# Phase 2 on row tiles with rings of four; residual and biases written to banks; new orders on all engines

## The reference

```python
# block 1: attention by exponential features, 16 heads of 8
q, k, v = split_heads(x@Wq.T+bq), split_heads(x@Wk.T+bk), split_heads(x@Wv.T+bv)
f = lambda t: exp((t/sqrt(8))@R - 0.5*sum((t/sqrt(8))**2))
out = einsum(f(q), einsum(f(k), v), 1/(sum(f(q)) + 1e-8)) @ Wo.T + bo
# block 2: 16 slots ask x, one expert per slot, then x asks the slots
o = slot + mha(slot, x, x; d_*)                       # 16 heads, 256 keys
h = layernorm(o)*g + b                                # each slot its own g, b
o = o + (silu(h@W1+b1) * silu(h@Wg+bg)) @ W2 + b2     # each slot its own weights
out = mha(x, o, o; c_*)                               # 16 heads, 16 keys
```

## Time and profile before

| | us |
|---|---|
| median of 3 runs | 195.14 (194.88 to 195.6) |
| profiled execution | 194.75 |
| its span in the trace | 193.0 |
| TensorE busy | 179.7 (93%) |
| GpSimd busy | 146.3 (76%) |
| VectorE busy | 141.6 (73%) |
| ScalarE busy | 116.6 (60%) |

### The profile page before, as it was taken

The page is one execution under the profiler, slowest core; times in us unless marked ns, Lnnn a source line. Parts: engine busy times, 40 slices in busy tenths (PEclk is TensorE's granted clock), DMA queues, the critical chain, the costliest instruction groups (busy, mean ns, idle before and its releaser), DMA issues.

```text
span 193.0 us, 4707 instructions
## 1 busy us (share of the span) xinstructions
PE 179.7 (93%) x1439; PEld 136.6 (71%) x1439; DVE 141.6 (73%) x413; ACT 116.6 (60%) x296; POOL 146.3 (76%) x286
## 2 busy tenths in 40 slices
PE   0898789999999999999999999999999799999993
PEld 0445477777876687777788767523777699999993
DVE  2669968788877887869785743655448999999961
ACT  2235367796688857867966675446334465666561
POOL 4498969879699985999277693317947999999960
PEclk9999999999999999999999999999999999999999
DMA  4739957999990000000000000000000001111122
GB/s 108 240 102 366 360 147 257 349 362 327 372 298 13 0 3 2 3 0 3 0 3 0 2 5 0 3 0 0 3 0 0 3 27 54 58 58 54 38 75 82
DMA packets 19674, 18.24 MB, mean 95 GB/s; under 512 B 1289, under 2 KB 15458, under 8 KB 19650
## 3 DMA queue, kind: packets, MB, share of 16 engines
q1 hardware_dynamic: 18802, 17.35, 28.3%
q10 hardware_dynamic: 848, 0.59, 1.1%
HBM read 15.84 MB, written 2.10 MB: 93 GB/s over the span
## 4 chain that ended last, share of the span: by engine, by line
PE 80%; POOL 11%; DMA 3%; DVE 2%; issue 1%; ACTq 1%; ACT 1%; POOLq 0%; DVEq 0%
PE ps L1061 11%; PE ps L1133 7%; PE ps L1328 7%; PE ps L1300 7%; PE ps L1183 4%; PE ps L1171 4%; PE ps L1241 4%; PE ps L1114 4%; PE ps L1071 4%; PE ps L1318 4%; PE ps L1094 3%; PE ps L1309 3%; PE ps L1084 3%; DMA X<-in_L_attn_x_dram 3%; PE ps L1125 2%; PE ps L1104 2%
## 5 line engine op out<-in xcount | busy, mean ns | idle before, releaser
L1061 PE MATMUL ps<-Wproj,xnT 128*128 128x512 f32 x64 | 32.5, 633 | 0.9 <-ACT Wproj L515 0.5
L481 POOL TENSOR_TENSOR pr<-ft,rsm 128x256 f32<-128x256 f32 x32 | 19.3, 625 | 0.9 <-DVE rsm L970 0.9
L1061 PEld LDWEIGHTS ps<-Wproj,xnT 128*128 128x128 f32 x64 | 11.4, 198 | 9.9 <-issue 8.6
L1133 PE MATMUL ps<-XN2T,Ad 128*128 128x256 f32 x64 | 16.7, 384 | 0.1
L1328 PE MATMUL ps<-sq,prT 128*128 128x128 f32 x128 | 16.8, 275 | 0.0
L1300 PE MATMUL ps<-xnT,XN2T 128*128 128x256 f32 x64 | 16.5, 383 | 0.0
L429 POOL TENSOR_SCALAR xn<-X,nm,rs 128x127 f32<-128x127 f32 x32 | 14.7, 468 | 1.5
L1328 PEld LDWEIGHTS ps<-sq,prT 128*128 128x128 f32 x128 | 15.5, 192 | 0.0
L794 DVE TENSOR_REDUCE ss<-sq 128x64 f32<-128x512 f32 x16 | 10.9, 678 | 5.8 <-ACT sq L555 5.7
L654 ACT ACTIVATE ft<-ex 128x512 f32<-128x512 f32 x16 | 10.1, 630 | 8.3 <-POOL pr L481 7.1
L548 ACT ACTIVATE pr<-ps,nmax 128x256 f32<-128x256 f32 x32 | 14.9, 474 | 0.3 <-DVE nmax L833 0.2
(11 more groups left out here) (178 smaller groups left out, 508.6 us busy)
## 6 DMA issues: line engine op xcount, KB each, us to landing
W1s<-in_L_ffn_e_W_dram SPq DMA_DIRECT2D x4, 1024.0 KB, 8.0
Wgs<-in_L_ffn_e_Wg_dram SPq DMA_DIRECT2D x4, 1024.0 KB, 8.3
W2s<-in_L_ffn_e_W_dram SPq DMA_DIRECT2D x16, 256.0 KB, 8.3
out_dram<-V2s SPq DMA_DIRECT2D x16, 128.0 KB, 1.7
X<-in_L_attn_x_dram SPq DMA_DIRECT2D x3, 512.0 KB, 6.1
X<-in_L_attn_x_dram ACTq DMA_DIRECT2D x2, 128.0 KB, 2.6
X<-in_L_attn_x_dram ACTq DMA_DIRECT2D x1, 256.0 KB, 4.9
W<-in_L_ffn_e_b_dram SPq DMA_DIRECT2D x3, 32.0 KB, 1.8
```

The source lines that it names most:

```text
L481: last = pool.tensor_tensor(heads(at[:, k, j * HS:(j + 1) * HS], S), heads(ep[:, k, j * HS:(j + 1) * HS], S), over(rsm[:, k, j * H:(j + 1) ...
L1061: last = pe.matmul(banks(b)[:, j, :], xnT[:, k, j * P:(j + 1) * P], Wproj[:, :], start=True, stop=True)
L1133: last = pe.matmul(ps[:, 4, hf * NT:(hf + 1) * NT], Ad[:, hf * P:(hf + 1) * P], XN2T[:, b, :], start=True, stop=True)
```

## The change

- **Phase 2** no longer steps in lockstep: each engine has a written order of calls over blocks, and the buffers are rings of four (RING), laid into the experts' weights, which are no longer needed by then.
- The queries are projected for blocks 0 to 3 only. For the others the weights are folded: key_weights multiplies WqT by the packed keys of six blocks at a time, four row tiles of 32 partitions, each into a bank of its own, and the scores take XN2T as it is with the result KW.
- Values: value_weights does the same for four blocks at a time (VSET), 16 products of 32 partitions to 64 columns of the array each, in place of BDv @ W[CO] block by block. GpSimd packs keys and values (pack_keys, pack_values) instead of spreading them, and spreads keys only for blocks 1 to 3.
- The residual add of phase 2 is split: ScalarE copies the outputs (keep_outputs), GpSimd adds X (add_kept); only block 15 is still added by VectorE. VectorE also does half of the last scaling (scale_last).
- Keys: VectorE makes the first block straight from the bank (first_keys); ScalarE keeps the rest.
- slot + d_bo is written to banks 0 and 1 by VectorE from loaded copies; three of the eight hidden biases are copied to their banks by ScalarE (set_bias). The loads for that stand on SP behind the experts' weights.
- key_values makes only the four diagonal 32x32 tiles, and mask_kv spreads them.
- No negated means; 1e-8 is a ninth element of each head in ft, summed with the others.
- TensorE begins with products of the identity (warm). The orders of all engines in phase 1 are new.

The diff, cut to its core (the long lines of calls in full only for phase 2 and the start):

```diff
-QUERIES1 = 6
-QUERIES2 = 11
+QUERIES2 = 4
+KEY_SETS = ((QUERIES2, (QUERIES2 + NB) // 2), ((QUERIES2 + NB) // 2, NB))
+BANK_KW = (0, 1, 6, 7)
+RING = 4
+VSET = NB // 4
+BY_DVE = (15,)
...
-            rstd1(0); rstd1(1); apply1(1); rstd1(3); apply1(2); apply1(3); slot_rows(); other_masks(); add_bias(0)
-            add_bias(1); scale_features(0); add_bias(2); rstd1(5); scale_features(1); apply1(4); add_bias(3)
+            rstd1(0); rstd1(1); apply1(1); rstd1(3); apply1(2); apply1(3); scale_features(0); rstd1(5)
+            other_masks(); add_bias(0); add_bias(1); add_bias(2); apply1(4); scale_features(1); rstd2(0); apply2(0)
...
+            def in_tiles(to, what, mask, first, end):
+
+                return pool.tensor_tensor(to[:, first:end, :].rearrange("p b (h s) -> p b h s", s=S),
+                                          what[:, :, first:end].rearrange("p s b -> p b s").unsqueeze(2)
+                                          .broadcast_to([P, end - first, EG, S]),
+                                          mask[:, :].unsqueeze(1).unsqueeze(3).broadcast_to([P, end - first, EG, S]),
+                                          ALU.mult)
...
+            spread_keys(1); pack_keys(0); spread_keys(2); spread_keys(3); pack_keys(1); scale2(0); pack_values(0)
+            scale2(1); pack_values(1); pack_values(2); scale2(2); add_kept(0); add_kept(1); scale2(3); scale2(4)
...
-                sc.activation(ft[:, b % 2], ex[:, b % 2], ACT.Exp).then_inc(ft_ok, 1)
+                sc.activation(ft[:, b % 2, :, :, 0:DH], ex[:, b % 2].rearrange("p j (h d) -> p j h d", d=DH),
+                              ACT.Exp).then_inc(ft_ok, 1)
...
+            def set_bias(n):
+
+                i = 5 + n
+                sc.wait_ge(sg_ok, i - 4)
+                sc.activation(ps[:, BANK_UP[i], :], hbias[:, n, :], ACT.Copy).then_inc(bias_set, 1)
+
+            sc.wait_ge(h_in, 16 * 3 * EG)
+            tanh(0, 0); tanh(0, 1); tanh(1, 0); set_bias(0); tanh(1, 1); set_bias(1); tanh(2, 0); set_bias(2)
+            tanh(2, 1); act_columns(0); tanh(3, 0); act_columns(1); tanh(3, 1); act_columns(2); act_columns(3)
...
+            def slots_residual():
+
+                ve.wait_ge(slots_in, 16 * EG)
+                ve.wait_ge(ex_ok, NB)
+                for half in range(2):
+                    last = ve.tensor_tensor(ps[:, half, 0:2 * P].rearrange("p (g d) -> p g d", g=2),
+                                            slotr[:, 2 * half:2 * half + 2, :], under(d_bo_all[:, :], 2), ALU.add)
+                last.then_inc(slots_set, 1)
...
+            first_keys(); maxima2(0); shift2(0); maxima2(1); shift2(1); sums2(0); maxima2(2); norms2(0); shift2(2)
...
+            def warm(n):
+
+                pe.wait_ge(ident_ok, 1)
+                for _ in range(n):
+                    pe.matmul(ps[:, 2, 0:P], ident[:, :], ident[:, :], start=True, stop=True)
...
-                pe.matmul(ps[:, 6, NT:NT + P], WvP[:, :], gT[:, b % 2, :], start=True, stop=True).then_inc(kv_ok, 1)
+                for r in range(EG):
+                    last = pe.matmul(ps[r * Q:(r + 1) * Q, 6, NT:NT + Q], WvP[:, r * Q:(r + 1) * Q],
+                                     gT[:, b % 2, r * Q:(r + 1) * Q], start=True, stop=True)
+                last.then_inc(kv_ok, 1)
...
+            warm(5); turn_biases(); warm(1); turn_weights(); feature_weights(); warm(1); turn_xn(0)
+            turn_value_weights(); warm(1); project(0); turn_xn(1); project(1); key_sums(0); turn_xn(2)
...
+            def key_weights(c):
+
+                first, end = KEY_SETS[c]
+                pe.wait_ge(tile_k_ok, c + 1)
+                wait(pe, kw_ok, 2 * c)
+                for r in range(EG):
+                    tile = slice(r * Q, (r + 1) * Q)
+                    last = pe.matmul(ps[:, BANK_KW[r], 0:(end - first) * 64], WqT[tile, :],
+                                     tile_k[tile, first:end, :].rearrange("p b m -> p (b m)"), start=True, stop=True)
+                last.then_inc(kwp_ok, 1)
+
+            def value_weights(g):
+
+                pe.wait_ge(tile_v_ok, g + 1)
+                pe.wait_ge(kw_ok, 4)
+                wait(pe, vw_ok, g)
+                for i in range(VSET):
+                    for r in range(EG):
+                        tile = slice(r * Q, (r + 1) * Q)
+                        last = pe.matmul(ps[(r % 2) * 64:(r % 2) * 64 + 64, r // 2, i * P:(i + 1) * P],
+                                         tile_v[tile, g * VSET + i, :], W[tile, CO, :], start=True, stop=True)
+                last.then_inc(vwp_ok, 1)
...
+            scores2(0); scores2(1); key_weights(0); scores2(2); scores2(3); key_weights(1); scores2(4); turn_at(0)
+            value_weights(0); turn_at(1); scores2(5); outputs2(0); scores2(6); outputs2(1); turn_at(2)
+            value_weights(1); scores2(7); outputs2(2); turn_at(3); scores2(8); turn_at(4); outputs2(3); scores2(9)
```

More of the change, by code:

```diff
@@ L623, in _ @@
+            keep_slots(13); exp_scores(14); keep_xn2(15); keep_slot_values(14); keep_prT(14); keep_slots(14)
+            exp_scores(15); keep_slot_values(15); keep_prT(15); keep_slots(15); part2()
+            for b in range(QUERIES2):
                 keep_queries(b)
@@ L881, in _ @@
-            slot_outputs(2); maxima(15); slot_weights_of_sums(3); slot_heads(3); slot_outputs(3)
-            slot_weights_of_sums(4); slot_heads(4); slot_outputs(4)
+            stats1(0); moments1(0); center_weights(); set_biases(); spread_rotation(); stats1(1); apply_first()
+            center_values(); moments1(1); stats1(2); stats1(3); moments1(2); moments1(3); stats1(4); moments1(4)
+            norms_sq(0); exponents(0); stats1(5); moments1(5); sums(0); norms(0); norms_sq(1); exponents(1)
@@ L1220, in _ @@
                 last.then_inc(o_ok, 1)
-            for b in range(QUERIES1, QUERIES2):
+            for b in range(QUERIES2):
                 queries(b)
@@ L1238, in experts_in @@
                 pe.wait_ge(hT_ok, 1 + g // 2)
+                wait(pe, bias_set, 2 * g + u - 4)
                 w = (W1s, Wgs)[u]
@@ L1333, in _, with scores2 @@
-            for t in range(STEPS2):
-                step2(t)
-                if t == 3:
-                    for b in range(QUERIES2 + 3, NB):
-                        queries(b)
+            slot_keys_values(1)
+            def scores2(b):
+                if b == 0:
+                    pe.wait_ge(bdk0_ok, 1)
+                    pe.wait_ge(q2_ok, QUERIES2)
+                elif b < QUERIES2:
+                    pe.wait_ge(bdk_ok, b)
+                else:
+                    pe.wait_ge(kw_ok, 2 if b < KEY_SETS[0][1] else 4)
+                wait(pe, sx_ok, b - 1)
+                keys = BDk[:, b, :] if b < QUERIES2 else KW[:, :, b, :]
+                for j in range(2):
+                    last = pe.matmul(ps[:, 2 + b % 2, j * HS:(j + 1) * HS], XN2T[:, b, j * P:(j + 1) * P],
+                                     keys, start=True, stop=True)
+                last.then_inc(sp_ok, 1)
@@ new lines, in turn_at @@
+            def turn_at(b):
+                wait(pe, at_ok, b + 1)
+                if b == NB - 1:
+                    pe.wait_ge(at_last, 1)
+                wait(pe, atT_ok, b - 1)
+                for j in range(2):
+                    for hf in range(2):
+                        last = pe.transpose(ps[:, 4 + b % 2, hf * NT + j * P:hf * NT + (j + 1) * P],
+                                            at[:, b % RING, j * HS + hf * P:j * HS + (hf + 1) * P], ident[:, :])
+                last.then_inc(tt_ok, 1)
@@ new lines, in outputs2 @@
+            def outputs2(b):
+                wait(pe, atT_ok, b + 1)
+                pe.wait_ge(vw_ok, b // VSET + 1)
+                if b >= 2:
+                    on_dve = b - 2 in BY_DVE
+                    pe.wait_ge(ob_dve if on_dve else oc_ok, done(b - 2, on_dve))
+                for j in range(2):
+                    for hf in range(2):
+                        last = pe.matmul(ps[:, 6 + b % 2, j * P:(j + 1) * P], atT[:, b % RING, hf, j * P:(j + 1) * P],
+                                         VWs[:, hf, b, :], start=(hf == 0), stop=(hf == 1))
+                last.then_inc(op_ok, 1)
```

568 lines of the change are left out of this document (274 added, 294 removed).

## The result

The changed kernel takes **202.2 us** (median of 4 runs, 202.1 to 202.33); the kernel before, beside it, 195.06 (194.88 to 195.6). The ratio is 1.036, with an interval of 1.034 to 1.037: slower by 3.6%, where 186.5 was forecast. The profiled execution took 202.33, its span is 200.6.

What follows compares the result with a forecast made beforehand. TensorE was taken to bound phase 1 and lead phase 2, with VectorE and GpSimd close. 194.75 - 3.5 + 0.4 - 2.1 - 0.2 - 0.35 - 2.85 = 186.15, as a median 186.5 us; range 183 to 192.

Steps and rivals of the forecast that it cites:

- Startup: First 26 us: GpSimd and VectorE work removed, identity products added, exponents(2) moved ahead; 3.5 us gained, bounds 1 to 5.2.
- Rival B: Phase 2: row tiles gain nothing, six sets cost 20.5 us instead of 6.0; 201 us, slower; chance 0.06.
- 1 of clock: Start: earlier TensorE work puts part of the first project at the fast level; 1 us taken, of 0 to 1.8.
- 2.5 of idle: Start: exponents(2) ahead of center_slot_weights and residual(0) lets project(3) start sooner; 2.5 us of TensorE's idle time gained.
- Phase 1, steady, +0.4: 26 to 110 us, TensorE full: key-value column tiles cost 0.16 us more alone, 0.04 less beside slots; +0.4 in all.
- rival D: Phase 1: reading ft in runs of eight slows key_sums by up to 7 us; 193.5 us; chance 0.05.
- From the last slots to the experts, -2.1: Last slot_outputs to turn_xh(0): output product 1.55 us earlier and one query fewer, so turn_xh(0) starts 2.1 us earlier.
- The query, -0.6: Behind the output product: one query product fewer ahead of turn_xh(0), saving about 0.6 us.
- Experts and into phase 2, -0.55: turn_xh(0) to scores(0): bias products moved to ScalarE copies, -0.2 us; VectorE makes the first keys block in one step, -0.35.
- Phase 2, -2.85: First scores to the end: 45.9 us against 48.74, with TensorE and VectorE each at 45.4 and 0.5 added for waits.
- A: Phase 2: row tiles writing the same bank take turns, 0.87 us more per value set, 3.5 in all; 190.0 us; chance 0.15.
- Rival C: Start gives 1 instead of 3.5 us as another wait holds project(3), and switches fall badly, +1.5; 190.5 us; chance 0.15.

Runs made afterwards that it cites:

- e1: The changed kernel with the negated means made again and added on GpSimd, instead of subtracting the mean; 189.66 us, ratio 0.970.
- f3: e1 with TensorE's four queries and ScalarE's copies of them put back between the steps of the last slots; 188.3 us, ratio 0.965.
- g1: f3 with three more identity products where TensorE waits for BDR, between turn_weights and feature_weights; 188.41 us, ratio 0.966.
- f2: e1 without any of the eight identity products ahead of the first project; 189.43 us, ratio 0.971.
- f4: e1 with another order of the last two blocks of phase 2 on VectorE, ScalarE and GpSimd; 188.93 us, ratio 0.966.
- g3: f3 with key_values again one 128x128 product and VectorE's mask over 128 rows, instead of four column tiles; 191.87 us, ratio 0.983.

## Why the prediction was wrong, by its steps

**The step that failed** is the first line of **Startup**: "Removed: on GpSimd the mask of the slots' residual, and the negated means, 0.19 us in each of 16 chains". A removal was costed and what stands in its place was not: the mean is now subtracted in the step that added. The prediction's own rule for an operation that no row shows, bounds from both sides, wasn't put to it, because instruction, shape and count looked the same. With an upper bound it would have been seen at once what is at stake. GpSimd was busy for 66.18 of 84 us, so 17.8 us were free there; 51 of the 62 steps lie in that stretch, and 17.8 / 51 = 0.35 us more for each would fill it. The subtraction costs about that, 0.37. The engine need not even be full: in the kernel after it is busy for 77.57 of the 84 us, and TensorE already stands idle for 7.84. Worked out so, this would have been a rival for a slower kernel with a cause of its own.

**Rival B** gave 201, close to the 202.2 measured, but as a mechanism it is refuted: it wanted row tiles that run one after the other, 3.7 us a value set, and they take 1.03 to 1.10. The number agrees by chance.

**Startup, -3.5: measured 0.0 in e1, -1.2 in f3, -2.4 in g1.** Three terms. "Its start doesn't move" was wrong: project(0) went from 7.85 to 9.12 (after) and 9.54 (e1). VectorE now makes BDR ahead of apply_first and waits for the load of R (1.24 us in the kernel after, 1.75 in e1), so the products with BDR start at 6.40 and 6.82 for 6.31; and between them and project(0) stand two identity products, turn_xn(0) (once ahead of them) and the transposes of the value weights (once behind project(0)), 0.43 us each at the low level. Without any identity product (f2) project(0) still starts at 9.06. "1 of clock": 1.5 in the kernel after (2.25 us instead of 3.78), 0.2 in e1 (3.61), all of it in f4; it is a draw, not a term. "2.5 of idle": the exponents did free project(3), from project(2) to project(3) 4.21 us instead of 6.21, so 2.0; but 0.56 of it was lost up to project(4) in e1, and 2.23 in the kernel after (9.56 instead of 7.33), where GpSimd led by then. "All of it reaches the end" holds only while TensorE is full, and there it wasn't.

**Phase 1, steady, +0.4: small as forecast, but of the other sign and wrong in its parts.** The eleven blocks from project(4) to project(15) took 65.54 us before, 64.93 in e1 and 64.94 in f3 (73.81 in the kernel after). The tiles for the key values save 0.30 beside slots and cost nothing alone, where I had 0.04 and +0.16. With the whole product in the new order (g3) these blocks take 67.09, so the tiles gave 2.15 of them and the new order took 1.55 back; no run here has taken that order apart. key_sums takes 0.44 to 0.53 us from its start to the next in e1, 0.44 to 0.62 before: rival D, the read of ft in runs, fell.

**From the last slots to the experts, -2.1.** The output product starts 0.06 us after the last slot_outputs in the kernel after (129.09 to 129.15) and 0.04 in e1, where it was 1.71, so -1.65 for the 1.55: right. The query, -0.6, turned into +0.64 in e1 and +0.96 after, with the clock that fell; with the queries in f3's places it is -1.03.

**Experts and into phase 2, -0.55: measured -1.0** (18.62 and 18.63 for 19.62). Right in sign; no bias product and no wait took its place.

**Phase 2, -2.85: measured -1.32.** The key sets (0.85; measured 0.86 to 0.89 from start to start) and the value sets (1.07; 1.03) were nearly right, against rival A, who wanted 1.9 a value set. The scores behind a set take 0.97 to the next start instead of 0.87, so the six came to some 6.5 us, not 6.0. **A is refuted**, and with it, for these products, the rule of the Trainium skill (TensorEngine Tiling (Array Packing), Restrictions and Gotchas) that different row tiles can't access one bank at the same time: 16 products that share two banks, on different partitions of them, cost 1.03 where 16 column tiles cost 0.87. The key sets, each tile with a bank of its own, are no cheaper for it: 0.86 where the forecast counted 0.65 for 384 columns. In both the excess over the columns is about 0.2. What was mis-sized is TensorE's own list. From the first scores to the last outputs it was busy for 43.14 us (the stretch from 153.18 shown above), where I had 41.2; its idle time, 1.18, and the 3.1 behind it were as forecast. Of the 1.9, 0.5 is in the sets and 0.5 in outputs, which take 0.98 instead of 0.89 in some five of the sixteen blocks; the steady step is 2.20 in the others. The remaining 0.9 isn't attributed. VectorE, which I had as the equal of TensorE, was busy for 35.53 of the 44.32 and did not lead. At two places others lead: the first value set waits for ScalarE's copies of the key weights, whose banks it needs (147.59 to 149.11 in e1's chain), and over the last blocks the chain of the kernel after is GpSimd's scalings and additions, from 188.2 to 195.4.

**Rival C** (a start that gives 1, bad switches, 190.5) comes near e1's 189.66 in the number, not in the mechanism: project(3) was freed, and the switches were a gain. Had the subtraction not been there, the forecast would have missed by 3 us, inside its wide range (183 to 192) and outside the one it gave to its own mechanism (184 to 188.8).

## What to carry to other kernels

An edit that only changes an operation inside an instruction is a new instruction: cost it from a row of the same engine with the same operation, or bound it by the point at which that engine becomes the limit. On GpSimd, negate the small operand once and add. Work that fills a wait of TensorE may matter for its clock too: before moving it behind a wait, ask what keeps the engine busy, and read the granted clock of the stretch that follows, in more than one execution, because the same list can keep the level or lose it (f3 and g3).

## What the runs showed of the hardware

- GpSimd's two-operation instruction on 128x127 f32 takes 0.82 to 0.85 us with a subtraction first and 0.46 to 0.48 with an addition first (a multiplication second in both), whether the scalar is a strided column of the statistics or stands in a small tile; on VectorE both take 0.34.
- Products on row tiles of 32 rows run side by side: sixteen of 128 columns that share two banks in 1.03 us, four of 384 columns in banks of their own in 0.86 to 0.89, from start to start.
- Column tiles placed beside other column tiles save 0.30 us a block, and alone they cost the same as the whole product (1.05 us with its neighbours, both).
- The rise from the 1.2 to the 2.4 GHz level came at different moments in executions of one list, with 2.9 us between the earliest and the latest project(1) seen (11.24 in f4 and 14.11 in e1, 0.46 of it due to a load). In e1 a stretch with 5.18 us of work in 8 was followed by one with a granted clock of 0.72. In f3 and g3 TensorE had the same work in the 11 us up to turn_xh(0) (8.84 and 8.83 us of it); behind that f3 kept 1.00, and g3 had 0.57 over the next 8 us and lost 2.8.
